# Moving a per-channel average over partitions from TensorE to two small DMAs and VectorE

## What is computed

```python
out = irfft2(rfft2(x) * rfft2(filter))[..., :L, :L] + x * bias[:, None, None]   # layer 0
scores = jnp.einsum('bpsd,bptd->bpst', x, x) * inv_dim                          # layer 1
red = jnp.sum(scores * weights[None], axis=-1, keepdims=True)
y = x + red
mean = jnp.mean(y, axis=(0, 2, 3), keepdims=True)
var = jnp.var(y, axis=(0, 2, 3), keepdims=True)
y_hat = (y - mean) * jax.lax.rsqrt(var + BN_EPS)
return y_hat * gamma[None, :, None, None] + beta[None, :, None, None]
```

## Time and profile before

| what | value |
|---|---|
| median of 3 runs | 968.88 us (968.71 to 970.04) |
| the profiled execution | 968.82 us, span of its instructions 966.9 us |
| busy, share of the span | TensorE 98%, VectorE 78%, ScalarE 70%, GpSimd 69% |
| DMA engines | 75.8% busy, 235.73 MB |
| mean granted TensorE clock | 0.992 |

### The profile page before, as it was taken

The page is one execution under the profiler, slowest core; times in us unless marked ns, Lnnn a source line. Parts: engine busy times, 40 slices in busy tenths (PEclk is TensorE's granted clock), DMA queues, the critical chain, the costliest instruction groups (busy, mean ns, idle before and its releaser), DMA issues.

```text
span 966.9 us, 18768 instructions
## 1 busy us (share of the span) xinstructions
PE 944.4 (98%) x5436; PEld 829.1 (86%) x5436; DVE 749.8 (78%) x2335; ACT 681.3 (70%) x1088; POOL 671.5 (69%) x518
## 2 busy tenths in 40 slices
PE   7999999999999999999999999999999999999993
PEld 5888888888888888888888888888888888888882
DVE  2678878878878878878878778788788788788785
ACT  2547777777777777777777777777767767767756
POOL 2767767767767777777777777777777777777750
PEclk9999999999999999999999999999999999999996
DMA  7765877878878887877778877877787787787634
GB/s 217 263 207 181 273 232 258 275 215 267 274 227 258 277 242 243 274 253 235 271 247 238 274 243 246 271 262 224 274 251 235 278 264 230 271 271 226 226 113 174
DMA packets 73294, 235.90 MB, mean 244 GB/s; under 512 B 7232, under 2 KB 24128, under 8 KB 65088
## 3 DMA queue, kind: packets, MB, share of 16 engines
q1 hardware_dynamic: 73280, 235.73, 75.8%
HBM read 168.40 MB, written 67.31 MB: 244 GB/s over the span
## 4 chain that ended last, share of the span: by engine, by line
PE 95%; ACT 2%; DVE 1%; DMA 1%; POOL 0%; issue 0%; ACTq 0%; DVEq 0%
PE ps_c L483 36%; PE ps_u L483 31%; PE ps_z L483 27%; PE ps_avg L483 1%; ACT out_sb L458 1%; DMA toep_whole<-filters_padded 1%; ACT z_sb L458 0%; DVE z_sb L678 0%; DMA par<-params_in 0%; POOL zl L391 0%; DVE products L700 0%; ACT zh L467 0%; DVE zl L689 0%; DMA filters_padded<-z_sb 0%; DVE z_sb L611 0%
## 5 line engine op out<-in xcount | busy, mean ns | idle before, releaser
L391 POOL TENSOR_TENSOR zl<-z_sb,zh 128x1024 fp32r<-128x1024 f32 x126 | 301.7, 2394 | 207.9 <-ACT zh L467 207.9
L700 DVE CUSTOM_DVE_ANT_0 products<-z_sb,ps_c 128x256 bf16<-128x256 f32 x508 | 183.6, 418 | 158.3 <-PE ps_c L483 158.3
L483 PE MATMUL ps_z<-uh,toep 128*128 128x512 f32 x768 | 270.8, 407 | 0.1
L437 ACT ACTIVATE uh<-ps_u 128x1024 fp32r<-128x1024 f32 x127 | 130.4, 1027 | 197.4 <-PE ps_u L483 197.4
L458 ACT ACTIVATE out_sb<-z_sb,shift,gain 128x256 f32<-128x256 f32 x496 | 257.1, 592 | 6.6
L483 PE MATMUL ps_u<-toep,xh 128*128 128x256 f32 x1016 | 240.0, 317 | 2.3 <-POOL toep L369 2.2
L483 PE MATMUL ps_c<-zh,wh 128*128 128x512 f32 x508 | 197.9, 389 | 1.2 <-DVE zl L689 0.7
L483 PE MATMUL ps_c<-zh,wl 128*128 128x512 f32 x508 | 198.1, 390 | 0.0
L483 PE MATMUL ps_c<-zl,wh 128*128 128x512 f32 x508 | 197.7, 389 | 0.0
L483 PE MATMUL ps_u<-toep_whole,xt_sb 128*128 128x128 f32 x1016 | 195.0, 273 | 0.0
L711 DVE BATCH_NORM_STATS2 stat<-z_sb 128x6 f32<-128x256 f32 x512 | 179.3, 413 | 0.0
(11 more groups left out here) (63 smaller groups left out, 924.9 us busy)
## 6 DMA issues: line engine op xcount, KB each, us to landing
xt_sb<-xt_in SPq DMA_DIRECT2D x64, 1024.0 KB, 9.3
x_sb<-x_in SPq DMA_DIRECT2D x128, 512.0 KB, 7.2
out<-out_sb SPq DMA_DIRECT2D x124, 512.0 KB, 3.5
w_sb<-wt_in SPq DMA_DIRECT2D x64, 256.0 KB, 6.7
toep_whole<-filters_padded SPq DMA_DIRECT2D x64, 256.0 KB, 6.5
out<-z_sb SPq DMA_DIRECT2D x4, 512.0 KB, 3.0
par<-params_in SPq DMA_DIRECT2D x1, 224.0 KB, 4.6
par<-params_in SPq DMA_DIRECT2D x1, 194.0 KB, 2.6
```

What stands on the lines that cost most here:

```text
L391: nc.gpsimd.tensor_tensor(zl[:, zs.slot(2)], z_sb[:, r, h], zh[:, zs.slot(2)].bitcast(F32), ALU.subtract)\
L437: nc.scalar.activation(uh[:, us.slot(2)], u_bank(us)[:, :, :, :], ACT.Copy)\
L483: return nc.tensor.matmul(o, a, b, start=start, stop=stop)
L700: last = nc.vector.tensor_tensor_reduce(products[:, cs.slot(2), k, b], z_sb[:, r, h, k, b], bank[:, k, b], 1.0 / math.sqrt(SIDE), 0.0, ALU ...
```

## The change

Per channel the two moments of every partition (`own`, 128 x 2) are written by a DMA from ACT's queue into a row of 256 numbers in DRAM (L455 of the changed kernel, step s for the channel of s-6), and one step later a second DMA from ACT's queue reads that row into all 128 partitions (L460, `everyone`). DVE takes batch statistics of the 128 means and the sum of the 128 variances one step after that (`totals`, now in the normalizing step, L642 to L652). The average matmul is gone from the loop. The last channel still uses TensorE, with two matmuls in place of three.

```diff
+        own_dram = nc.dram_tensor("partition_moments", [XR, 2 * P], F32, kind="Internal")
...
-            def inverse_deviation(vs, reads):
+            def inverse_deviation(vs):
...
-                pool.wait_ge(averages_read, reads)
+                wait_chan(pool, veps_ready, vs, 1)
...
+                ms = st.trail(LAG_MEAN)
+                if starts(ms) and not ending(ms, 2):
+                    r = ms.ring(XR)
+                    wait_chan(act, mean_in, ms, 1)
+                    nc.scalar.dma_start(own_dram[r:r + 1, :].rearrange("o (p n) -> (o p) n", n=2), own[:, r])\
+                        .then_inc(gathered, 16)
+                ss = st.trail(LAG_SPREAD)
+                if starts(ss) and not ending(ss, 2):
+                    act.wait_ge(gathered, ss.channel(1) * 16)
+                    nc.scalar.dma_start(everyone[:, ss.ring(2), 0:2 * P],
+                                        bass.AP(own_dram, ss.ring(XR) * 2 * P, [[0, P], [1, 2 * P]]))\
+                        .then_inc(spread[ss.ring(2)], 16)
...
-                ms = st.trail(LAG_MEAN)
-                if starts(ms):
-                    wait_chan(pe, mean_in, ms, 1)
-                    wait_chan(pe, moment_in, ms, 0)
-                    wait_chan(pe, averages_read, ms, 0)
-                    average(ms.ring(XR))
...
+            def totals(vs):
+
+                e, r = vs.ring(2), vs.ring(XR)
+                dve.wait_ge(spread[e], vs.turn(2) * 16)
+                everyones = everyone[:, e].rearrange("p (n two) -> p two n", two=2)
+                nc.vector.bn_stats(mean_stat[:, e], everyones[:, 0, 0:P]).then_inc(mean_stat_ready, 1)
+                nc.vector.tensor_reduce(var_sum[:, e], everyones[:, 1, :], mybir.AxisListType.X, ALU.add)\
+                    .then_inc(var_sum_ready, 1)
+                wait_chan(dve, mean_stat_ready, vs, 1)
+                nc.vector.memset(spacer[:, :], 0.0)
+                nc.vector.bn_aggr(mean_var[:, e], mean_stat[:, e]).then_inc(totals_ready, 1)
+                wait_chan(dve, totals_ready, vs, 1)
+                wait_chan(dve, var_sum_ready, vs, 1)
+                nc.vector.tensor_scalar(veps[:, r], var_sum[:, e], 1.0 / P, mean_var[:, e, 1:2],
+                                        ALU.mult, ALU.add).then_inc(veps_ready, 1)
+                nc.vector.tensor_scalar(neg_mean[:, r], mean_var[:, e, 0:1], -1.0, None, ALU.mult)\
                     .then_inc(neg_mean_ready, 1)
...
             def stage(st):
-                vs = st.trail(LAG_SPREAD)
+                vs = st.trail(LAG_TOTAL)
                 if starts(vs):
-                    wait_chan(dve, averaged, vs, 1)
-                    read_mean(vs)
-                    variance(vs.trail(2))
-                    second_moment(vs)
+                    totals(vs)
...
             whole_z(end[1])
+            totals(Step(0, PAIRS - 6))
             gain_and_offset(Step(0, PAIRS - 8))
             mean_of_partition(before)
...
-            dve.wait_ge(averaged, CH - 1)
-            read_mean(before)
-            variance(before.trail(2))
-            second_moment(before)
             statistics(end[1])
-            gain_and_offset(before.trail(2))
-            dve.wait_ge(averaged, CH)
-            variance(before)
+            gain_and_offset(Step(0, PAIRS - 6))
+            totals(before)
+            gain_and_offset(before)
             reduce_rows(end[1], ps_u)
-            gain_and_offset(before)
```

More of the change, by code:

```diff
@@ L45 @@
 LAG_MEAN = 6
-LAG_SPREAD, LAG_POWER, LAG_NORM = 7, 9, 10
+LAG_SPREAD, LAG_TOTAL, LAG_POWER, LAG_NORM = 7, 8, 9, 10
 LAG_LOAD_XT, LAG_LOAD_T, LAG_LOAD_W, LAG_LOAD_X = 1, 3, 3, 5
@@ L175, in build @@
         stat = sb("stat", [P, XR, GROUPS, 6])
-        avg_in = sb("avg_in", [P, XR, 3])
+        own = sb("own", [P, XR, 2])
+        everyone = sb("everyone", [P, 2, 2 * P + 2])
+        mean_stat = sb("mean_stat", [P, 2, 6])
+        mean_var = sb("mean_var", [P, 2, 2])
+        var_sum = sb("var_sum", [P, 2, 1])
+        last_moment = sb("last_moment", [P, 1])
         neg_mean = sb("neg_mean", [P, XR, 1])
@@ L198, in build @@
         ps_c = ps("ps_c", [P, BLOCKS, PAIR, SIDE])
-        ps_avg = ps("ps_avg", [P, 2])
+        ps_avg = ps("ps_avg", [P, 3])
         first_landed = sem("first_landed")
@@ L233, in build @@
         neg_mean_ready = sem("neg_mean_ready")
-        averages_read = sem("averages_read")
+        gathered = sem("gathered")
+        spread = [sem(f"spread{i}") for i in range(2)]
+        mean_stat_ready = sem("mean_stat_ready")
+        var_sum_ready = sem("var_sum_ready")
+        totals_ready = sem("totals_ready")
+        veps_ready = sem("veps_ready")
         rstd_ready = sem("rstd_ready")
@@ L336, in _ @@
             nc.gpsimd.memset(minus_half[:, :], -0.5).then_inc(const_ready, 1)
-            nc.gpsimd.memset(avg_in[:, :, :], 0.0).then_inc(const_ready, 1)
+            nc.gpsimd.memset(everyone[:, :, 2 * P:2 * P + 2], P * BN_EPS).then_inc(const_ready, 1)
             pool.wait_ge(const_ready, 4)
@@ L358, in stage @@
                 if starts(vs) and not ending(vs, 4):
-                    inverse_deviation(vs, vs.channel(2))
+                    inverse_deviation(vs)
                 ms = st.trail(LAG_MEAN)
@@ L583, in _ @@
             product_c(end[0], ps_c)
[L584 to L587, removed]
             product_c(end[1], ps_u)
[L590 to L598, removed]
+            pe.wait_ge(mean_in, CH)
+            mm(ps_avg[:, 0:2], ones[:, :].bitcast(F32), own[:, (CH - 1) % XR], True, True).then_inc(averaged, 1)
+            pe.wait_ge(moment_in, 1)
+            mm(ps_avg[:, 2:3], ones[:, :].bitcast(F32), last_moment[:, :], True, True).then_inc(averaged, 1)
         @block.vector
@@ L632, in _ @@
                                     ALU.mult).then_inc(filt_ready, 1)
-            def read_mean(vs):
-                nc.vector.tensor_scalar(neg_mean[:, vs.ring(XR)], ps_avg[:, 1:2], -1.0, None, ALU.mult)\
-                    .then_inc(neg_mean_ready, 1)
[L639 to L652, removed]
+            def totals(vs):
[13 more added lines that the diff above has]
+                nc.vector.tensor_scalar(neg_mean[:, r], mean_var[:, e, 0:1], -1.0, None, ALU.mult)\
+                    .then_inc(neg_mean_ready, 1)
             def gain_and_offset(vs):
                 r = vs.ring(XR)
+                wait_chan(dve, neg_mean_ready, vs, 1)
                 wait_chan(dve, rstd_ready, vs, 1)
@@ L668, in mean_of_partition @@
                 nc.vector.memset(spacer[:, :], 0.0)
-                nc.vector.bn_aggr(avg_in[:, r, 1:3], stat[:, r].rearrange("p g s -> p (g s)"))\
+                nc.vector.bn_aggr(own[:, r], stat[:, r].rearrange("p g s -> p (g s)"))\
                     .then_inc(mean_in, 1)
@@ L757, in _ @@
             reduce_rows(end[0], ps_c)
-            dve.wait_ge(averaged, CH - 1)
-            read_mean(before)
-            variance(before.trail(2))
-            second_moment(before)
             statistics(end[1])
-            gain_and_offset(before.trail(2))
-            dve.wait_ge(averaged, CH)
-            variance(before)
+            gain_and_offset(Step(0, PAIRS - 6))
+            totals(before)
+            gain_and_offset(before)
             reduce_rows(end[1], ps_u)
-            gain_and_offset(before)
             mean_of_partition(final)
[L769 to L774, removed]
+            r = final.ring(XR)
+            dve.wait_ge(averaged, 1)
+            nc.vector.tensor_scalar(neg_mean[:, r], ps_avg[:, 0:1], -1.0, None, ALU.mult)\
+                .then_inc(neg_mean_ready, 1)
+            nc.vector.tensor_scalar(var_sum[:, 1], ps_avg[:, 1:2], BN_EPS, None, ALU.add).then_inc(var_sum_ready, 1)
+            dve.wait_ge(neg_mean_ready, CH)
+            nc.vector.tensor_scalar(dev[:, r], own[:, r, 0:1], neg_mean[:, r], None, ALU.add).then_inc(dev_ready, 1)
+            dve.wait_ge(dev_ready, 1)
+            nc.vector.tensor_scalar(last_moment[:, :], dev[:, r], dev[:, r], None, ALU.mult).then_inc(moment_in, 1)
+            dve.wait_ge(averaged, 2)
+            dve.wait_ge(var_sum_ready, CH)
+            nc.vector.tensor_scalar(veps[:, r], ps_avg[:, 2:3], var_sum[:, 1], None, ALU.add).then_inc(veps_ready, 1)
             gain_and_offset(final)
-            r = final.ring(XR)
             dve.wait_ge(offset_ready, CH)
```

8 lines of the change are left out of this document (2 added, 6 removed).

## The result

The changed kernel takes **1037.83 us** (median; 1034.5 to 1039.92) beside 969.2 us for the kernel before: 1.0701 of its time, 95% interval 1.0689 to 1.0714. It is slower by 68 us. The forecast was 959.3 us, faster by 1%, and its range ended at 985.

What follows compares the result with a forecast made beforehand. TensorE, busy 98% of the span, was taken to bound the kernel. From 968.8 us, 13.6 came off for the average, 3.0 was added for the longer loop and 1.1 for the tail: 959.3 us, range 955 to 985.

Steps and rivals of the forecast that it cites:

- TensorE gives back 13.6 us: On TensorE in the loop: dropping the average saves 0.22 us per channel, for 62 averages, 13.6 us.
- T = 1.10 us: On DVE ahead of gain: the six instructions of totals take 1.10 us, bounds 0.9 to 1.8.
- G = 0.35: On ACT ahead of shift: issuing the write takes 0.35 us, bounds 0.33 and 0.61.
- the room of 1.51: In the normalizing chain: totals plus the write's issue may take 1.51 us before TensorE waits.
- the excess of 3.0 us: In the loop: the longer chain overruns its room by 0.05 us per channel over 59 channels, 3.0 us.
- Rival (1): At the write ahead of shift: the chain over ACT becomes the bound, for example 991 us; chance 16%.
- It is 128 KB in a queue of its own, so I take 4 to 5 us: in time, by little: Broadcast on ACT's queue: lands in 4 to 5 us, inside a window of 6.1 us before totals wants it.
- so I cost it at nothing: Write to DRAM: has about 7 us before ACT waits for it; nearest row landed in 1.9 us; cost nothing.
- Rival (2): At totals on DVE: the broadcast lands late and sets the period; 980 to 1022 us, say 1000; chance 14%.
- The tail, +1.1 us: After the loop: 1.75 us added ahead of the second last `zh`, 0.63 saved on four reads; +1.1 us.
- SP's loads ... I cost that at nothing: On SP: a step's loads go out 1.7 us later, but two steps or more before use; cost nothing.
- What would show it wrong: Signs: `ps_c` waiting for `zl` by several tenths, DVE idle before statistics of `everyone` on DMA, clock falling in the loop.

Runs made afterwards that it cites:

- e3: Changed kernel with totals reading a constant tile and both DMAs (write and broadcast) left out; 956.17 us, 0.9859 of the kernel before.
- e7: Changed kernel with totals on a constant tile, no broadcast, and the write waited for only by the write two channels later; 958.59 us, 0.988.
- e8: Changed kernel with SP issuing the normalizing step's loads only after the next step's `uh` is done; 1067.74 us, 1.0993 of the kernel before.
- e4: Changed kernel with a broadcast of 8 bytes per partition in place of 1 KB, the rest of the tile constant; 1011.02 us, 1.0416.
- e1: Changed kernel with totals run one step later (lag 9 in place of 8); 966.38 us, 0.996 of the kernel before.
- e2: Changed kernel with totals reading a constant tile; both DMAs still issued and ACT still waiting for the write; 974.1 us, 1.005.
- e9: e1 with the broadcast issued at the end of ACT's step, totals behind `z_sb` and POOL's power just ahead of `zl`; 956.98 us, 0.9871.

## Why the prediction was wrong

**TensorE gives back 13.6 us: right.** With nothing late (e3) the gain is 0.0141 x 969.2 = 13.7 us. From one `ps_c` to the `ps_c` two steps on, e3 takes 14.23 us as a median, as predicted. In the changed kernel itself two steps in which TensorE hardly waits take 14.25: the first matmuls of three successive `ps_c` start at 482.16, 489.28 and 496.41.

**T = 1.10 us: too long; G = 0.35: right.** Totals starts at 480.91 and `gain` at 481.76, T = 0.85; the issue of the write takes 0.33. Their sum of 1.18 is under the room of 1.51, so the excess of 3.0 us in the sum isn't there. Rival (1) falls by e3 for the arithmetic and by e7 for the write's issue on top of it. This term made the forecast too slow; the ones below made it too fast.

**"It is 128 KB in a queue of its own, so I take 4 to 5 us: in time, by little": this step failed.** The broadcast's wait stood in the sum with nothing, and DVE waited 72.6 us for it. Measured: 7.8 us median, 3.2 to 10.8. A queue of its own gave it no way past the loads. The price that I did have in the rows, 6.5 to 7.2 us for loads that queue behind others, was the nearest one, and I set it aside because a store of 512 KB lands in 3.5. But SP issues that store ahead of the step's loads, where the broadcast goes out among or behind them: e8 shows 2.9 us ahead of them and 9.2 behind them. Size was the wrong measure (e4: 7.3 us with 1 KB); what was issued before it is the right one. The window, for its part, was wider than I said: the broadcast goes out at 487.48, when `uh` begins and not when it ends, and DVE comes to totals at about 495.0 (496.09 less 1.10 of waiting), 7.5 us later instead of 6.1. It would have held 4 to 5 us easily, and didn't hold 7.8. e1 shows it from the other side: with one step of slack the time is 71 us less.

The Trainium skill, page "DMA: Bandwidth & Descriptors", section "Issuing engines are not separate DMA queues", says that transfers issued by different engines share the same 16 DMA engines and interleave. The trace agrees: once the broadcast moves, packets of both queues fall in the same microsecond (85 of q1 and 13 of q10 from 492 to 493). The same page's "Queues, rings and completion order" has each DMA engine alternate between the issuers' rings. Taken by itself that would have the broadcast start at once beside the loads. It didn't: no packet of ACT's queue for over 4.5 us, with the DMA engines 1% to 53% busy from 488 to 492. The page may still hold for a DMA engine that has work from both queues; what keeps the broadcast's work from it for so long, no run here shows.

**The write, "so I cost it at nothing": this failed too.** It was priced with a transfer that had nothing else in flight. Under load it lands in 4.4 us as a median and up to 8.2, and in 7.0 to 7.2 in e1 and e2. The cover of "about a step (7 us)" was 4.8 us as the code stands (482.72 to 487.48). My text did name what would happen ("ACT stands with `zh` behind it") and gave it no price. It costs twice: directly, as part of the 16.5 us between e7 and e2, and by making ACT issue the broadcast late, which goes with 13 of the 17 periods of 16.3 to 20.3 us. That the second is the larger part of the loss is read from the trace of the change; no run took the write's lateness away alone at this lag.

**Rival (2): the right mechanism, with 14% and 980 to 1022 us, say 1000; measured 1038.** Its chain from landing to the next issue was 8.1 us and measured 6.57, its decision point 6.1 and measured 7.5. At the median landing it gives now 6.57 + 7.8 = 14.4, almost no loss. The loss is in the spread around the median, which I left out: a late write adds its lateness to the period, and by the slip other loads stand ahead of this broadcast and the next: after 4 of the 13 late writes the next period too was over 16 us, although its own write landed in under 3. What this shift does to TensorE (standing for `ul`, then a clock of 0.55) comes on top. I didn't measure how much of the loss the clock makes.

**The tail, +1.1 us: about right.** From the start of the last `ps_u` matmul (toep_whole with xt_sb) to the end of the span it is 32.37 us before and 33.23 after, +0.9. **"SP's loads ... I cost that at nothing"** held in e3. **What would show it wrong** held word for word: DVE idle before the statistics of `everyone` with the DMA as releaser, and a clock that falls in the loop.

Left open: where the order between the two queues is kept, at the making of descriptors or in the DMA engines (the runs show the order, not the place). Also why e1, whose totals do depend on the broadcast, is 0.9% faster than e2, whose totals don't; in e1 totals is out of the normalizing step, where e2 has both totals and ACT's wait, but this was not tried by itself. And why a write lands now in 4 and now in 8 us: in the change it takes 2.6 to 4.3 us with at most two of SyncE's transfers in flight, but anything from 4.0 to 8.2 with three.

## What to carry to other kernels

Price a small DMA by what has been issued ahead of it on all queues, not by its bytes and not by the queue it goes on: take the landing time of the neighbours in the backlog. In a loop paced by one engine, a DMA round trip through DRAM can be nearly free (e9 at 956.98 us and e3 at 956.17 can't be told apart here) if each landing has a whole step of slack and its wait stands behind the step's urgent work; at less slack look at the spread of its landing, since the worst ones set the periods. A wait for a DMA on an engine that also issues the next DMA moves that one back in the backlog, and the delay can reach the next round.

## What the runs showed of the hardware

- A transfer that ScalarE issues behind loads of SyncE starts late, although it has a queue of its own: 2.9 us to landing ahead of a group of loads, 9.2 behind it (e8), and over 4.5 us without a packet while the DMA engines had room (the change). The order is nearly kept in the landings, not strictly: in the change 195 of the 205 transfers of SyncE that were in flight when a broadcast was issued landed before it; in e9, where a store goes out 0.5 us ahead of the broadcast, 52 of the stores landed after it.
- 128 rows of 8 bytes to DRAM slow the store around them: 512 KB land in 7.0 us instead of 3.6, and SyncE's queue takes 82.1% of the DMA engines' time instead of 76.7% for the same 235.73 MB (DMA views of e7 and e3). Of the 32768 packets of 4 KB, 881 took over 0.5 us each in e7 and 104 in e3.
- Small statistics are cheap: 0.29 us for 128 elements, and 0.85 us for all six instructions of totals.
- Issuing a transfer of 128 rows holds ScalarE's queue for 0.33 us.
